# The last keys of four batches packed into three V tiles, and the output projections of attention 1 one round sooner

## The chip, the cores and the metric

The kernel runs on one core of a Trainium2 chip. The metric is the device time of one execution in microseconds (us). The engines are named as in the profile: PE (TensorE, matrix products), PEld (its weight loads), DVE (VectorE), ACT (ScalarE), POOL (GpSimd) and SP (SyncE, which here only issues DMAs). Each engine runs its own list of instructions in order and waits on semaphores.

## The reference, cut to what matters

Two layers of gated cross attention and feed-forward act on x, which is 8 batches x 100 rows x 512. The keys and values come from a context of 8 batches x 722 keys x 512, with 16 heads of width 32.

```
k = heads(ctx @ Wk.T + bk)         # 722 keys a batch
v = heads(ctx @ Wv.T + bv)
p = softmax(q @ k.T / sqrt(32))    # attention 0 adds a mask
x = x + tanh(g) * (p @ v)          # attention 1: (p @ v) @ Wo.T + bo
x = x + tanh(f) * ffn(layernorm(x))
```

722 keys are five tiles of 128 and one of 82.

## The kernel before

The program runs attention 0, a ternary feed-forward of 88 weight units, attention 1 and a quantized feed-forward of 7 row tiles. Products of fp32 numbers are made from a high and a low half in the type fp32r: high by high, high by low and low by high, so one product over 512 inputs is 4 x 3 = 12 matmuls.

**Rounds.** Each attention works through 64 pairs of heads, 8 for each batch. In round i PE issues `scores(i+1)` (four matmuls, lines 850 to 855), `turn(i)` (twelve transposes of the weights of pair i, L866), the jobs of `beside(i)`, and `weigh(i-1)` (six matmuls of the turned weights with V, L888; L881 in the last batch of attention 0). The table `BESIDE` at line 64 says which jobs stand in which of the 8 rounds of a batch. A job `("v", x, kt)` makes tile kt of V for the batch x further on (L806, 128 keys as the stationary operand, 512 moving columns). A job `("k", x, g, half)` makes a part of the keys (L802). Before the change, the first entry is `(("v", 0, 5), ("k", 0, 3, 1))`: the tile of the last 82 keys of this batch, then a K job.

**The other engines in round i.** DVE: `peak` twice (L1293, the maxima of the scores), `low_weighed(i-2)` (L1314, L1318), `low_turned(i)` (L1299, three pieces), then the low halves of the jobs (`low_job`, L1281 for K, L1285 for V). ACT: `high_weighed(i-2)` (L1845), `high_turned(i)` (L1830), `weights` twice (L1818, exponentials) and the high halves of the jobs (`high_job`, L1786 and L1799). A job's PSUM bank comes out of a ring of two banks which it shares with `weigh` and others. `ring_free` waits until the item two places back has been read. The second score matmul of a round waits for both exponentials of the round before. POOL makes the low halves of the context (L2179). SP issues the loads in an order written out by hand.

**Extras in attention 0.** From round 17 on, in rounds with i % 8 = 1, PE turns a normalized batch (`turn_normal`, L929), DVE runs `low_weighed` ahead of `peak`, and `normal_out` (L1416) stands at the end of the round before.

**The end of attention 1.** `OUT_AT` at line 126 puts `project(n)` (12 matmuls with Wo, L1003) for row tiles n = 0 to 5 into rounds 58 to 63, where no jobs are left. Around it stand ACT `high_out(n)` (L1861), POOL `low_out(n)` (L2205), POOL `add_bo(n)` (L2212), DVE `add_projected(n)` (L1349, which waits for `project(n)` and for `add_bo(n)`) and `stats_projected(n)` (L1357, L1359). POOL splits Wo beforehand (`high_wo`, `low_wo`, L2197 and L2200). DVE `scale_rows(n)` (from L1370 or L1375) prepares the quantized rows. `turn_rows(0)` (L1015) is the first step of the feed-forward on PE. It stands in round 63 and waits for the second piece of `low_turned(63)`, and the rest of PE's list stands behind it.

## Time and profile before

| | |
|---|---|
| median of 3 runs | 1589.43 us (1589.24 to 1590.16) |
| the profiled execution's own time | 1589.02 us |
| its span in the trace | 1587.1 us |
| PE, PEld | 1572.9 us (99%), 1431.8 us (90%) |
| DVE, ACT, POOL | 1021.3 us (64%), 968.2 us (61%), 401.6 us (25%) |
| chain that ended last | PE 92%, DVE 4%, DMA 2% |

"Busy" is the time covered by at least one record of the engine. Records of matmuls overlap, so what a matmul costs is the time from its start to the start of the next one. A line of the timeline has the start in us, the duration, the engine, the source line, the operation, what it writes and reads, the shape and a count. In brackets stands the idle time of the engine before it and what ended it.

### The profile page before, as it was taken

The numbers are of one execution on the slowest core, as the hardware profiler recorded it, in microseconds if no ns is written. First come the engines' busy times: TensorE is split into PE (matmuls) and PEld (weight loads), VectorE is DVE, ScalarE is ACT, GpSimd is POOL, SyncE is SP. The second block draws the span as 40 slices with busy tenths as digits, with TensorE's granted clock in tenths as the row PEclk, the third lists the DMA queues.
The fourth block names the chain that finished last, engine by engine and source line by source line (L and its number), as shares of the span: only waits on it lengthen the run. The fifth ranks groups of instructions, "written<-read, shape, count | busy, mean of one in ns | idle before, by whom it ended". The sixth has DMA issues, their size and how long they took to land.

```text
span 1587.1 us, 25783 instructions
## 1 busy us (share of the span) xinstructions
PE 1572.9 (99%) x9370; PEld 1431.8 (90%) x9370; DVE 1021.3 (64%) x1807; ACT 968.2 (61%) x2006; POOL 401.6 (25%) x545
## 2 busy tenths in 40 slices
PE   9999999999999999999999999999999999999999
PEld 7899899989988999999999998889989889998765
DVE  6577787787785562223544425647777777777987
ACT  5566767677765455544544435357667667766676
POOL 4111211212144222222222222311102111113751
PEclk9999999999999999999999999999999999999999
DMA  8766776676582325554375643576676676658500
GB/s 249 176 166 173 184 187 180 156 201 174 140 209 85 105 81 194 175 190 160 104 230 193 221 156 97 171 183 183 151 195 164 163 178 176 177 132 222 183 13 30
DMA packets 146966, 258.15 MB, mean 163 GB/s; under 512 B 40944, under 2 KB 91248, under 8 KB 146701
## 3 DMA queue, kind: packets, MB, share of 16 engines
q1 hardware_dynamic: 146497, 256.10, 57.7%
q8 instruction: 86, 1.41, 0.4%
q14 instruction: 51, 0.42, 0.1%
q10 hardware_dynamic: 332, 0.23, 0.0%
HBM read 187.86 MB, written 58.57 MB: 155 GB/s over the span
## 4 chain that ended last, share of the span: by engine, by line
PE 92%; DVE 4%; DMA 2%; issue 1%; ACT 1%; SPq 0%; POOL 0%; DVEq 0%; ACTq 0%
PE ps L1152 33%; PE ps L806 17%; PE ps L802 15%; PE ps L888 8%; PE ps L866 8%; PE ps L1086 2%; PE ps L954 2%; PE ps L850 2%; PE ps L855 2%; PE ps L1103 1%; PE ps L853 1%; PE ps L854 1%; PE ps L1003 1%; DMA KS<-kd 1%; DVE PT L1299 1%
## 5 line engine op out<-in xcount | busy, mean ns | idle before, releaser
L1152 PE MATMUL ps<-ah_f,wh_f 128*128 128x400 f32 (+1 forms) x1296 | 442.9, 343 | 0.0
L1152 PE MATMUL ps<-al_f,wh_f 128*128 128x400 f32 (+1 forms) x1296 | 442.2, 342 | 0.0
L2179 POOL TENSOR_TENSOR cxl<-raw,cxh 128x384 fp32r<-128x384 f32 (+1 forms) x112 | 105.7, 965 | 613.8 <-ACT cxh L1775 613.8
L1697 DVE TENSOR_TENSOR wl_f<-raw_f,wh_f 128x1024 fp32r<-128x1024 f32 x85 | 103.7, 1223 | 232.7 <-POOL wh_f L2169 232.6
L1152 PEld LDWEIGHTS ps<-al_f,wh_f 128*128 128x128 f32 x1296 | 243.8, 188 | 0.0
L1152 PEld LDWEIGHTS ps<-ah_f,wh_f 128*128 128x128 f32 x1296 | 243.5, 188 | 0.1
L1293 DVE TENSOR_REDUCE nmax<-ps 100x1 f32<-100x722 f32 x256 | 220.7, 903 | 32.5 <-PE ps L854 29.1
L1818 ACT ACTIVATE P<-ps,nmax 100x722 f32<-100x722 f32 x256 | 220.2, 862 | 29.7 <-DVE nmax L1293 29.4
L1830 ACT ACTIVATE PT<-ps 128x400 fp32r<-128x400 f32 x384 | 165.9, 505 | 70.6 <-PE ps L866 69.5
L2097 ACT ACTIVATE raw_f<-wl_f 128x1024 f32<-128x1024 f32 x88 | 93.4, 1061 | 174.6 <-DVE wl_f L1697 174.5
L1299 DVE TENSOR_TENSOR PT<-ps,PT 128x400 fp32r<-128x400 f32 x384 | 196.3, 566 | 4.3 <-ACT PT L1830 1.1
L2169 POOL CAST wh_f<-raw_f 128x1024 fp32r<-128x1024 f32 x85 | 92.8, 1092 | 334.4 <-PE ps L1152 323.7
L802 PE MATMUL ps<-cxh,wkh 128*128 128x338 f32 (+1 forms) x512 | 173.3, 338 | 0.7 <-DVE cxl L1271 0.7
L802 PE MATMUL ps<-cxh,wkl 128*128 128x338 f32 (+1 forms) x512 | 168.4, 329 | 0.0
L802 PE MATMUL ps<-cxl,wkh 128*128 128x338 f32 (+1 forms) x512 | 167.6, 327 | 0.0
L806 PE MATMUL ps<-wvh,cxh 128*128 128x512 f32 (+1 forms) x384 | 159.1, 414 | 0.9 <-DVE V L1281 0.9
L866 PE MATMUL ps<-ident,P 100*128 100x100 f32 (+1 forms) x1536 | 153.1, 249 | 1.3 <-DVE PT L1299 1.3
L866 PEld LDWEIGHTS ps<-ident,P 100*128 100x128 f32 (+1 forms) x1536 | 143.0, 137 | 12.0 <-ACT P L1818 1.5
L888 PE MATMUL ps<-PT,V 128*128 128x400 f32 x720 | 150.9, 344 | 0.6 <-DVE ksl L1281 0.6
L806 PE MATMUL ps<-wvh,cxl 128*128 128x512 f32 (+1 forms) x384 | 151.1, 393 | 0.0
L806 PE MATMUL ps<-wvl,cxh 128*128 128x512 f32 (+1 forms) x384 | 150.6, 392 | 0.0
L1281 DVE SCALAR_TENSOR_TENSOR ksl<-ps,cols,ksh 128x384 fp32r<-128x384 f32 (+1 forms) x120 | 71.0, 591 | 112.9 <-ACT ksh L1786 112.9
(218 smaller groups left out, 2592.3 us busy)
## 6 DMA issues: line engine op xcount, KB each, us to landing
KS<-kd SPq DMA_DIRECT2D x192, 361.0 KB
raw_f<-in_h SPq DMA_DIRECT2D x64, 512.0 KB, 4.5
raw_f<-in_gud SPq DMA_DIRECT2D x48, 512.0 KB, 4.6
raw<-in_ctx SPq DMA_DIRECT2D x64, 192.0 KB, 3.7
raw_f<-in_w SPq DMA_DIRECT2D x24, 512.0 KB, 3.7
kd<-ksh SPq DMA_DIRECT2D x60, 192.0 KB, 2.2
kd<-ksl SPq DMA_DIRECT2D x60, 192.0 KB, 2.5
raw<-in_ctx SPq DMA_DIRECT2D x64, 169.0 KB, 4.2
```

What stands on the lines that cost most here:

```text
L802: ins = e.matmul(o, m.wk[x][:, k, 128 * j[2]:128 * j[2] + 128], m.cx[y][:, k, off:off + n], start=(k == 0 and c == 0), stop=(k == 3 and c ...
L806: ins = e.matmul(o, m.cx[y][:, k, 128 * kt:128 * kt + KM[kt]], m.wv[x][:, k, :], start=(k == 0 and c == 0), stop=(k == 3 and c == 2))
L866: ins = e.transpose(ps[0:KM[kt], bank, o:o + S], m.P[0:S, (2 * i + h) % 3, 128 * kt:128 * kt + KM[kt]], ident[0:S, 0:S])
L888: ins = e.matmul(o, m.V[b % 2][0:r, kt, g, 128 * pr:128 * pr + 128], m.PT[0:r, i % 2, :, kt, :], start=(kt == 0), stop=(kt == KT - 1))
L1152: return e.matmul(o, p, q, start=start, stop=stop)
L1293: e.tensor_reduce(m.nmax[0:S, c:c + 1], scores_of(n), AX.X, ALU.max, negate=True).then_inc(v_max, 1)
L1299: e.tensor_tensor(lo, ps[:, bank, 0:400].rearrange("p (k n) -> p k n", k=2), raw32(hi), ALU.subtract).then_inc(v_t, 1)
L1697: e.tensor_tensor(wl[:, z, :], raw[:, r, :], raw32(wh[:, z, :]), ALU.subtract).then_inc(v_ul, 1)
L1818: e.activation(m.P[0:S, n % 3, :], scores_of(n), ACT.Exp, bias=m.nmax[0:S, c:c + 1], accum_out=m.rs[0:S, r:r + 1]).then_inc(a_exp, 1)
L1830: e.activation(m.PT[:, i % 2, 0, 2 * x:2 * x + 2, :], ps[:, bank, 0:400].rearrange("p (k n) -> p k n", k=2), ACT.Copy).then_inc(a_t, 1)
L2097: e.activation(raw[:, r, :], raw32(wl[:, z, :]), ACT.Abs, accum_out=low[:, z, 0:1]).then_inc(a_raw, 1)
L2179: e.tensor_tensor(m.cx[1][:, k, off:off + n], m.raw[:, k, off:off + n], raw32(m.cx[0][:, k, off:off + n]), ALU.subtract).then_inc(g_cx, 1)
```

## The change

1. The job `("v", 0, 5)` leaves the first round of a batch. In the second round (i % 8 = 1) a new `tail_job` stands ahead of `("v", 1, 0)`, for batches with b % 4 < 3. Its stationary operand of 114, 128 or 114 keys holds the last keys of this batch and of the next one (`PIECES`), so four batches need three jobs. `weigh(8b)`, the last step of the same round, waits for it.
2. The host lays the tails out in a new input. SP loads a tile (`load_tail`, 128 x 512 numbers) in the last round of the batch before, POOL splits it in the first round (`split_tail`, a cast and a subtraction), ACT and DVE write the result to V in two pieces each (`high_tail`, `low_tail`), since the rows go to two V buffers. From batch 1 on, the tile stands in the buffer of the raw context. SP therefore waits for the tail job before it loads the context of batch b + 2.
3. `OUT_AT` starts at round 57. `STATS_AFTER`, `OUT_FIRST`, the root and normalization steps on POOL and `scale_rows` on DVE move by one round with it. POOL's `add_bo(0)` and `add_bo(1)` stay in round 57.

```diff
-BESIDE = [(("v", 0, 5), ("k", 0, 3, 1)),
+BESIDE = [(("k", 0, 3, 1),),
+def tail_at(i):
+    return i // 8 if i < NP and i % 8 == 1 and i // 8 % 4 < 3 else None
+PIECES = (((0, 0, 0, 82), (96, 1, 64, 82)),
+          ((0, 0, 0, 64), (64, 1, 0, 64)),
+          ((96, 0, 64, 82), (0, 1, 0, 82)))
+TAIL_ROWS = (114, 128, 114)
...
-OUT_AT = {58 + i: i for i in range(TILES - 1)}
-STATS_AFTER = (59, 60, 61)
-OUT_FIRST = (60, 62)
+OUT_AT = {57 + i: i for i in range(TILES - 1)}
+STATS_AFTER = (58, 59, 60)
+OUT_FIRST = (59, 61)
...
+                    if p == 7 and tail_at(i + 2) is not None:
+                        load_tail(L, m, b + 1)
...
                     if p in (1, 5) and b + 2 < B:
+                        if p == 1 and b:
+                            w.wait_ge(p_job, tail_done(L, b))
...
+                def tail_job(b):
+                    j = ("v", b, KT - 1)
+                    ring_free(j)
+                    w.wait_ge(g_tail, 2 * (6 * L + tail_of(b)) + 2)
+                    r, o = TAIL_ROWS[b % 4], job_out(m, j, ring_bank(L, j))
+                    for k in range(4):
+                        wait_low_w(w, L, 4 + k)
+                        n = 128 * (k % 2)
+                        for c, (x, y) in enumerate(PAIRS):
+                            ins = e.matmul(o, m.tail[min(b, 1)][y][:, k // 2, n:n + r], m.wv[x][:, k, :],
+                                           start=(k == 0 and c == 0), stop=(k == 3 and c == 2))
+                    ins.then_inc(p_job, 1)
...
-                    w.wait_ge(v_job, NJOB * L + JOB[L]["v", b, KT - 1] + 1)
+                    w.wait_ge(v_job, tail_done(L, b))
...
+                def low_tail(b):
+                    j = ("v", b, KT - 1)
+                    w.wait_ge(a_job, NJOB * L + JOB[L][j] + 1)
+                    for v, o in tail_parts(m, b, ring_bank(L, j)):
+                        ins = e.tensor_tensor(v[:, :, 1:3, :], o, raw32(v[:, :, 0:4:3, :]), ALU.subtract)
+                    ins.then_inc(v_job, 1)
...
-                    if L and i == 61:
+                    if L and i == 60:
                         scale_rows(0)
+                    if L and i == 62:
+                        scale_rows(1)
                     if L and i == 63:
                         inverse(B - 1)
-                        scale_rows(1)
...
-                    if L and i == 60:
+                    if L and i == 59:
                         normal(0)
-                    if L and i == 62:
+                    if L and i == 61:
                         quantize(0)
                     if L and i + 1 in OUT_AT:
                         low_out(OUT_AT[i + 1])
-                    if L and i == 60:
+                    if L and i == 59:
                         tile_roots(1)
                     if L and i == 57:
                         add_bo(0)
-                    if L and (57 <= i < 61 or i == 62):
-                        add_bo(min(i - 56, 5))
+                        add_bo(1)
+                    if L and 58 <= i < 62:
+                        add_bo(i - 56)
...
+                def high_tail(b):
+                    j = ("v", b, KT - 1)
+                    w.wait_ge(p_job, NJOB * L + JOB[L][j] + 1)
+                    w.wait_ge(p_pv, NP * L + 8 * b)
...
+                    for v, o in tail_parts(m, b, ring_bank(L, j)):
+                        ins = e.activation(v[:, :, 0:4:3, :], o, ACT.Copy)
+                    ins.then_inc(a_job, 1)
...
+                def split_tail(b):
+                    (high, low), new = m.tail[min(b, 1)], m.tail_raw[min(b, 1)]
+                    w.wait_ge(d_tail, 16 * (6 * L + tail_of(b) + 1))
+                    if b:
+                        wait_ctx(w, L, b + 1, 0, 3)
+                    e.tensor_copy(high, new).then_inc(g_tail, 1)
+                    w.wait_ge(g_tail, 2 * (6 * L + tail_of(b)) + 1)
+                    e.tensor_tensor(low, new, raw32(high), ALU.subtract).then_inc(g_tail, 1)
...
-                    w.wait_ge(p_job, 2 * NJOB - 1)
+                    w.wait_ge(p_job, NJOB + JOB[1]["v", B - 1, KT - 2] + 1)
```

**Where instructions move.** The first place is DVE in rounds 16 and 17 of attention 0, before: from the maxima of round 16 to the end of round 17.

```order
138 L1293 TENSOR_REDUCE nmax_57<-ps 100x1 x2
139 L1314 TENSOR_TENSOR sum_65<-ps,sum_65 64x200
140 L1318 TENSOR_TENSOR QT_68<-ps,sum_65 32x100 x2
141 L1299 TENSOR_TENSOR PT_64<-ps,PT_64 128x2x200 x3
142 L1285 TENSOR_TENSOR V_0_60<-ps,V_0_60 82x4x128
143 L1281 SCALAR_TENSOR_TENSOR ksl_72<-ps,cols,ksh_71 128x338
144 L1416 TENSOR_SCALAR x_100<-x_100,mv,rq 100x512
145 L1314 TENSOR_TENSOR sum_65<-ps,sum_65 64x200
146 L1318 TENSOR_TENSOR QT_68<-ps,sum_65 32x100 x2
147 L1293 TENSOR_REDUCE nmax_57<-ps 100x1 x2
148 L1299 TENSOR_TENSOR PT_64<-ps,PT_64 128x2x200 x3
149 L1285 TENSOR_TENSOR V_0_61<-ps,V_0_61 128x4x128
```

The same place after the change, from the K job of round 16 on.

```order
144 L1347 SCALAR_TENSOR_TENSOR ksl_72<-ps,cols,ksh_71 128x338
145 L1490 TENSOR_SCALAR x_108<-x_108,mv,rq 100x512
146 L1388 TENSOR_TENSOR sum_65<-ps,sum_65 64x200
147 L1392 TENSOR_TENSOR QT_68<-ps,sum_65 32x100 x2
148 L1367 TENSOR_REDUCE nmax_57<-ps 100x1 x2
149 L1373 TENSOR_TENSOR PT_64<-ps,PT_64 128x2x200 x3
150 L1359 TENSOR_TENSOR V_0_60<-ps,V_0_60 18x4x128
151 L1359 TENSOR_TENSOR V_0_61<-ps,V_0_61 82x4x128
152 L1351 TENSOR_TENSOR V_0_61<-ps,V_0_61 128x4x128
```

The 82-row piece has left round 16, and two pieces of 18 and 82 rows stand in round 17 behind the maxima.

The second place is POOL in rounds 56 to 58 of attention 1, before.

```order
387 L2197 CAST woh<-wos 128x512 x4
388 L2200 TENSOR_TENSOR wol<-wos,woh 128x512 x4
389 L2205 TENSOR_TENSOR otl_116<-QT_93,oth_115 128x460
390 L2212 TENSOR_TENSOR xr<-xr,bo_123 115x512 x2
391 L2205 TENSOR_TENSOR otl_118<-QT_93,oth_117 128x460
392 L2212 TENSOR_TENSOR xr<-xr,bo_123 115x512
```

And after the change.

```order
411 L2301 CAST woh<-wos 128x512 x4
412 L2304 TENSOR_TENSOR wol<-wos,woh 128x512 x4
413 L2309 TENSOR_TENSOR otl_124<-QT_97,oth_123 128x460
414 L2309 TENSOR_TENSOR otl_126<-QT_97,oth_125 128x460
415 L2316 TENSOR_TENSOR xr<-xr,bo_131 115x512 x2
```

The low half of output tile 1 now stands between that of tile 0 and the addition of the bias to rows 0 and 1.

The third place is DVE behind the turned weights of rounds 62 and 63 of attention 1. Before, from the turned weights of round 63 on.

```order
1008 L1299 TENSOR_TENSOR PT_89<-ps,PT_89 128x2x200 x3
1009 L1327 RECIPROCAL rr_80<-rs_81 100x16
1010 L1370 TENSOR_SCALAR hs<-xr,mv,rq 115x512
1011 L1375 TENSOR_REDUCE ax<-hs 115x1
1012 L1377 TENSOR_SCALAR ax<-ax 115x1
1013 L1378 TENSOR_SCALAR ax<-ax 115x1
1014 L1380 RECIPROCAL ax<-ax 115x1
1015 L1382 TENSOR_SCALAR ax<-ax,tot 115x1 x2
1016 L1384 TENSOR_SCALAR ax<-ax 115x1
1017 L1349 SCALAR_TENSOR_TENSOR xr<-ps,gt,xr 115x512
1018 L1357 BN_STATS st<-xr 115x6
1019 L1359 BN_AGGR mv<-st 115x2
```

After the change, from the first step behind the turned weights of round 62 up to those of round 63.

```order
1015 L1449 TENSOR_REDUCE ax<-hs 115x1
1016 L1451 TENSOR_SCALAR ax<-ax 115x1
1017 L1452 TENSOR_SCALAR ax<-ax 115x1
1018 L1454 RECIPROCAL ax<-ax 115x1
1019 L1456 TENSOR_SCALAR ax<-ax,tot 115x1 x2
1020 L1458 TENSOR_SCALAR ax<-ax 115x1
1021 L1423 SCALAR_TENSOR_TENSOR xr<-ps,gt,xr 115x512
1022 L1431 BN_STATS st<-xr 115x6
1023 L1433 BN_AGGR mv<-st 115x2
1024 L1388 TENSOR_TENSOR sum_94<-ps,sum_94 64x200
1025 L1392 TENSOR_TENSOR QT_97<-ps,sum_94 32x100 x2
1026 L1373 TENSOR_TENSOR PT_93<-ps,PT_93 128x2x200 x3
```

`scale_rows(1)`, `add_projected(5)` and its statistics have moved ahead of the turned weights of round 63.

## Rows read from the trace of the kernel before

**Rows 1.** The page: busy time, share and instructions of each engine

```profile
PE 1572.9 (99%) x9370; PEld 1431.8 (90%) x9370; DVE 1021.3 (64%) x1807; ACT 968.2 (61%) x2006; POOL 401.6 (25%) x545
```

**Rows 2.** Timeline of PE, attention 0: a K job of 338 columns, a V job

```profile
153.16 0.32 PE L802 MATMUL ps<-cxh,wkh 128*128 128x338 f32 x1
...
155.03 1.25 PE L888 MATMUL ps<-PT,V 128*128 128x400 f32 x6
...
158.18 0.47 PE L806 MATMUL ps<-wvh,cxh 128*128 128x512 f32 x1
...
161.04 1.25 PE L888 MATMUL ps<-PT,V 128*128 128x400 f32 x6
```

**Rows 3.** Timeline of attention 1, round 9, which has one V job

```profile
1124.28 0.39 PE L850 MATMUL ps<-KS,QS 96*100 96x512 f32 x1
...
1124.90 1.73 DVE L1293 TENSOR_REDUCE nmax<-ps 100x1 f32<-100x722 f32 x2 [0.37 <-PE ps L854]
...
1127.52 0.86 ACT L1818 ACTIVATE P<-ps,nmax 100x722 f32<-100x722 f32 x1
1127.64 1.54 DVE L1299 TENSOR_TENSOR PT<-ps,PT 128x400 fp32r<-128x400 f32 x3
...
1128.77 1.26 PE L888 MATMUL ps<-PT,V 128*128 128x400 f32 x6
1128.97 0.60 ACT L1799 ACTIVATE V<-ps 128x512 fp32r<-128x512 f32 x1 [0.51 <-PE ps L806]
1129.60 0.69 DVE L1285 TENSOR_TENSOR V<-ps,V 128x512 fp32r<-128x512 f32 x1 [0.42 <-ACT V L1799]
1129.87 0.40 PE L850 MATMUL ps<-KS,QS 96*100 96x512 f32 x1
```

**Rows 4.** Timeline of attention 1, rounds 57 and 58: the second score matmul waits

```profile
1460.89 0.85 ACT L1818 ACTIVATE P<-ps,nmax 100x722 f32<-100x722 f32 x1
...
1461.89 0.34 PE L853 MATMUL ps<-KS,QS 96*100 96x210 f32 x1 [0.37 <-ACT P L1818]
```

**Rows 5.** Timeline of attention 0, rounds 0 to 2

```profile
59.18 0.39 PE L850 MATMUL ps<-KS,QS 98*100 98x512 f32 x1
...
60.62 1.72 DVE L1293 TENSOR_REDUCE nmax<-ps 100x1 f32<-100x722 f32 x2
...
65.17 1.76 ACT L1775 ACTIVATE cxh<-raw 128x384 fp32r<-128x384 f32 x4
...
71.65 0.39 PE L850 MATMUL ps<-KS,QS 98*100 98x512 f32 x1
```

**Rows 6.** Timeline of DVE, attention 0, rounds 16 and 17

```profile
177.18 0.54 DVE L1416 TENSOR_SCALAR x<-x,mv,rq 100x512 f32<-100x512 f32 x1
...
178.73 1.73 DVE L1293 TENSOR_REDUCE nmax<-ps 100x1 f32<-100x722 f32 x2
```

**Rows 7.** Timeline of attention 1, rounds 56 to 58, around the first output tile

```profile
1450.23 0.40 PE L850 MATMUL ps<-KS,QS 96*100 96x512 f32 x1
...
1457.32 5.00 POOL L2200 TENSOR_TENSOR wol<-wos,woh 128x512 fp32r<-128x512 f32 x4
...
1462.39 1.09 POOL L2205 TENSOR_TENSOR otl<-QT,oth 128x460 fp32r<-128x460 f32 x1
...
1463.44 2.55 POOL L2212 TENSOR_TENSOR xr<-xr,bo 115x512 f32<-115x512 f32 x2
```

**Rows 8.** Stretch: length; busy PE, PEld, DVE, ACT, POOL; clock, DMA share, GB/s

```profile
1467.50:1484.60 17.10, 17.10 (x108) 14.60 (x107) 16.14 (x34) 12.78 (x31) 14.01 (x29) 1.00 0.95 323
```

**Rows 9.** Timeline of DVE and PE, attention 1, rounds 58 to 64

```profile
1466.63 0.75 DVE L1349 SCALAR_TENSOR_TENSOR xr<-ps,gt,xr 115x512 f32<-115x512 f32 x1
...
1495.96 0.36 PE L1015 MATMUL ps<-idb,xq 115*128 115x115 bf16 x4
...
1496.37 0.46 DVE L1370 TENSOR_SCALAR hs<-xr,mv,rq 115x512 f32<-115x512 f32 x1
...
1499.96 0.33 DVE L1314 TENSOR_TENSOR sum<-ps,sum 64x200 f32<-64x200 f32 x1
```

More of the change, by code:

```diff
@@ L438, in job_out @@
                 return ps[:, bank, 0:HALF[j[3]][1]]
-            return ps[0:KM[j[2]], bank, :]
+            return ps[0:TAIL_ROWS[j[1] % 4] if j[2] == KT - 1 else KM[j[2]], bank, :]
         def ring_bank(L, item):
@@ L2352, in attention @@
                 low_q(0)
+                split_tail(0)
                 low_ctx(1, 0)
@@ L2355, in attention @@
                     b, p = divmod(i, 8)
+                    if i and tail_at(i + 1) is not None:
+                        split_tail(b)
                     if scaled_at(i + 1) is not None:
@@ L2457, in col @@
         return v.reshape(-1, 128).T
+    tails = np.zeros((6, 128, 4, 128), np.float32)
+    for b in range(B):
+        for o, x, r0, r1 in PIECES[b % 4] if b % 4 < 3 else ():
+            keys = I["ctx_1024"][b + x, 640 + r0:640 + r1, :]
+            tails[tail_of(b), :, :, o:o + r1 - r0] = keys.reshape(r1 - r0, 4, 128).transpose(2, 1, 0)
+    tails = tails.reshape(6, 128, 512)
     a = {
```

63 lines of the change are left out of this document (51 added, 12 removed).

## The prediction, made before the changed kernel was run

> **What bounds the kernel now.** I read the page first: PE has a record in work for 99% of the span [rows 1], so time comes off only where PE has less to do. The records overlap, so I priced PE's work by starts. A V job runs from 158.18 to 161.04, where the next kind of matmul starts: 2.86 us for 12 matmuls, of which 0.07 is a longer first slot that its successor has anyway. I take 2.8 us, or 0.23 us a matmul. The 338-column K job takes 155.03 - 153.16 = 1.87 us, and I take 1.84 [rows 2]. The stationary operand may be 82 keys or 128, the 512 columns stream either way.
>
> Then I read one round as a clock, from its first score matmul [rows 3]. The maxima start at +0.62 and end at +2.35. The second exponential runs from +3.24 to +4.10. `weigh` starts at +4.49 behind one V job and the next round at +5.59. So scores and turns take 4.49 - 2.8 = 1.69 us and `weigh` 1.10. A round without jobs would take PE 2.8 us, but the exponentials end at +4.10, so about 4.1 us is the least length of a round. PE starts 0.15 us after the exponential it waited for: 1461.89 against 1460.89 + 0.85 [rows 4]. With these two numbers I see which round becomes too short.
>
> Last comes the end of attention 1. There DVE is busy 16.14 of 17.10 us [rows 8]. It is as much a bound there as PE.
>
> **What is removed.** Per attention 8 tail jobs become 6, so 4 jobs go: 4 x 2.8 = **-11.2 us**. The Trainium skill (TensorE: Matmul & The Clock Gate, Back-to-back issue gap) gives 131 ns per matmul of 512 columns as a sustained rate. By it the four jobs would be worth 4 x 12 x 0.131 = 6.3 us (an estimate by that page). The trace has 0.23 us for this very matmul, and the trace decides.
>
> **Rounds with i % 8 = 0** lose 2.8 us and keep the K job: 1.69 + 1.84 + 1.10 = 4.63 us, above 4.1. They still cover the exponentials, by 0.5 us. `weigh` starts at +3.53 here, and its bank is free when DVE has done `low_weighed`. That one ends where the turned weights start: 1127.64 - 1124.28 = +3.36 [rows 3], plus 0.15 makes 3.51. It just fits. I take 0, with up to 0.1 in each of 14 rounds (+1.4) as the upper bound.
>
> **Tail rounds (i % 8 = 1).** The tail job ends at +4.49, the V job behind it at +7.29, then `weigh` waits for the tail. ACT starts its first piece at +4.69 (0.20 after the job, as 1128.97 against 1128.77), the second 0.49 later, and ends at +5.78. DVE starts at +5.81 and needs two pieces, 0.61 + 0.69 since neighbours overlap by 0.08: +7.11. With 0.15 PE is free at +7.26, against +7.29 [rows 3]. I price a piece of 18 rows like one of 128, as rows do not shorten these operations. So 0 for the six plain cases (batches 1, 2, 4, 5, 6 of attention 1 and batch 1 of attention 0), with up to 0.2 each (+1.2) as the upper bound. POOL's two new operations and SP's load end well ahead: the split takes about 2 us in a round in which POOL has nothing else, and SP's new wait delays only a context load that is used five rounds later.
>
> The Trainium skill (GPSIMD Engine Reference, 1. Specifications) says that POOL shares its SBUF interfaces with VectorE, with contention for DVE instructions with two SBUF inputs. The DVE steps of a round read at least one operand from PSUM, so I put no price on it.
>
> **Attention 0, batches 2, 4, 5 and 6.** `normal_out` used to start 0.18 after the next round's scores (177.18) and the maxima at 178.73, 1.73 after them [rows 6]. In the shorter round it follows the K job and starts at 5.25 - 4.64 = +0.61 of the next one. The maxima end at 0.61 + 1.55 + 1.73 = +3.89, the exponentials with the accumulator's read-out at +5.73. Now ACT is late for the tail: pieces until +6.82, DVE until +8.15, PE free at +8.30. `weigh` is due at 7.29 + 0.34 for the extra transposes = 7.63. That is 0.67 each: **+2.7 us** (0 to 3.6).
>
> **Batch 0 of both attentions.** The maxima of round 1's scores start late, at 60.62 - 59.18 = +1.44, behind a V piece, and end at +3.16 [rows 5]. The exponentials end at 3.16 + 0.03 + 0.85 + 0.86 = +4.90, so the second score matmul comes at +5.05. Without V job and `weigh`, PE gets there at 1.69 + 1.84 + 0.23 = +3.76. It waits 1.3 us. Behind the exponentials ACT has the K copy, four context copies (1.76, [rows 5]), about 1.3 for the turned weights and two exponentials, until +10.4. The tail's copies end at +11.5, DVE's at +12.8, PE goes on at +12.95, while it was due at +12.2. The round after starts at 12.95 + 1.10 = 14.05. Before, it was 71.65 - 59.18 = 12.47 with the same number of jobs. So +1.6 each, **+3.1 us** (1 to 4).
>
> **The last batch of attention 0.** Round 56 shrinks as well and `normal_out` delays the first maximum by 0.45 us, in a stretch whose rounds are bounded by the exponentials: **+0.5 us** (0 to 1).
>
> **The end of attention 1.** I count from the scores at 1450.23. Before: the first `add_projected` starts at 1466.63 (+16.4) and `turn_rows(0)` at 1495.96 (+45.7) [rows 7, 9]. These 29.3 us are DVE's work.
> - After, round 57 starts at +4.64. POOL finishes Wo about 2.5 us sooner than before, as the V tile that it waits for is no longer last: 1462.32 - 1450.23 - 7.3 = +4.8 (before it started behind the tail job, now behind the scaling of bo). The low half of tile 0 ends near +6.6 and PE waits 0.35 us for it.
> - Tile 1's high half comes behind the exponentials of round 57, until +9.6. POOL needs 1.09 for its low half and only then adds the bias to row tile 0, 1.3: +12.0 [rows 7]. `add_projected(0)` waits for that and DVE stands still for 2.4 us.
> - From +12.05 DVE has the 29.3 us of before, one more round of maxima, weighed and turned pieces (1129.18 - 1124.90 = 4.3, [rows 3]), and `scale_rows(1)` with `add_projected(5)` and its statistics (1499.96 - 1496.37 = 3.6, [rows 9]), which used to stand behind. That makes +49.2 for `turn_rows(0)`, with PE idle for some 5 us before it.
>
> So this stretch is 3.5 us longer, though it holds 2.8 us less of V job. Behind it PE was the bound, and at most 0.1 comes back. Stall: 3.5 + 2.8 - 0.1 = **+6.2 us** (3 to 7.5).
>
> **Sum.** -11.2 + 2.7 + 3.1 + 0.5 + 6.2 = +1.3 us on the profiled execution's 1589.0: 1590.3. The median of the runs lies 0.4 above that execution, so I predict **1590.7 us**.
>
> **Rivals.**
> - *The tail is paid for, no more.* DVE catches up at the end, or POOL's bias step is not what holds it, so that 6.2 shrinks to 1 or less, and the smaller waits stay: -11.2 + 2.7 + 3.1 + 0.5 + 1 = -3.9, 1585.5. With half of the smaller waits gone as well, about 1582.5. For it: PE was busy 17.10 of 17.10 us in the stretch [rows 8], so something there did fit around DVE. Against it: DVE's share. Chance 0.27.
> - *The thin margins open (the slower side).* In the rounds of 4.63 us `low_weighed` decides at 3.51 against 3.53, in the tail rounds DVE's second piece at 7.26 against 7.29. From 0.05 us of delay on, each such round stalls. At 0.1 and 0.2 that is 1.4 + 1.2 = 2.6, with the end at its upper bound 1.3 more: 1594.6. Chance 0.25.
> - *A matmul is cheaper than its slot*, so that removing one gives 0.131 us: -6.3 instead of -11.2, 1595.6. The spacing in [rows 2] is steady and without idle time, which speaks against it. It is the rule of the Trainium skill's page named above. Chance 0.01.
> - *The change does not do what it says*, for instance because PE starts waiting for `split_tail`. POOL is free and the load has a full round, so 0.01 more on the slower side.
>
> **Numbers.** My forecast, 1590.7, has 0.46. Its own range is 1587 to 1592.6. The range for eight in ten reaches to 1584 below (the first rival without its far end) and to 1595 above (the second). A measurement of this kernel can tell about 0.2% (3.2 us) from no change. Faster by more than that (below 1586.2) 0.27, within it 0.46, slower (above 1592.6) 0.27.
>
> **What would show it.** V rows of L806's kind should drop by 48 matmuls. Rounds with i % 8 = 0 should last 4.6 us. In attention 0, `weigh` should wait about 0.7 us for DVE in rounds 17, 33, 41 and 49. The waits of PE should have a new row of 4 to 5 us, `turn_rows(0)` behind DVE's turned weights. DVE should stand idle for 2 us or so before its first `add_projected`, released by POOL's bias step. If that last wait is missing, the forecast is too high by up to 6 us. If `weigh` waits in every tail round, it is too low.

## The result, and the profile after

The changed kernel takes 1597.26 us (median of 6 runs, 1595.13 to 1599.51). The kernel before took 1588.92 us (median of 6 runs, 1588.36 to 1590.16). The ratio is 1.0055, with a 95% interval of 1.0044 to 1.0066. So it is slower, by 8.3 us as the two medians have it (8.7 by the ratio). The prediction was 1590.7 us with a range of 1584 to 1595, so the measured time lies above the range. The profiled execution took 1597.67 us, its span in the trace is 1595.3 us, 8.2 us more than before.

The page of the changed kernel, busy time of each engine (answers [rows 1]):

```profile
PE 1568.5 (98%) x9322; PEld 1430.1 (90%) x9322; DVE 1026.4 (64%) x1815; ACT 971.1 (61%) x2014; POOL 424.0 (27%) x569
```

PE has 48 matmuls fewer (9322 against 9370) and is busy 4.4 us less than before, yet the span grew by 8.2. So PE waits where it did not wait before. The view of waits of PE shows where. Its two longest rows and that of the tails, over the whole span (what waits, what it waits for, us in total, times, longest):

```profile
PE ps L1079 <- DVE PT L1373: 5.0, 1, 5.0
PE ps L1067 <- DVE xr L1423: 2.8, 2, 2.2
...
PE ps L952 <- DVE V L1359: 1.7, 6, 0.4
```

`turn_rows(0)` waits 5.0 us for DVE's turned weights, as forecast. `project(1)` waits 2.2 us for DVE's first `add_projected`, which was not forecast. `weigh` waits for the tail in six rounds so long that PE stands idle. In the other six tail rounds it starts late as well, but by so little that the record before it still covers the wait (below).

Now the end of attention 1, from the scores at 1450.64 on (before they start at 1450.23, [rows 7]). KS is the tile of keys that the scores read, and it comes from memory through `kd`. PE:

```profile
1450.64 0.40 PE L914 MATMUL ps<-KS,QS 96*100 96x512 f32 x1
...
1465.49 0.48 PE L1067 MATMUL ps<-woh,oth 128*115 128x512 f32 x1 [2.25 <-DVE xr L1423]
...
1466.17 0.63 PE L1067 MATMUL ps<-woh,otl 128*115 128x512 f32 x1
1466.60 0.63 PE L1067 MATMUL ps<-woh,oth 128*115 128x512 f32 x1
...
1501.74 0.55 PE L1079 MATMUL ps<-idb,xq 115*128 115x115 bf16 x4 [4.99 <-DVE PT L1373]
...
1508.78 1.44 PE L952 MATMUL ps<-PT,V 128*128 128x400 f32 x6
```

DVE, POOL and SP's queue in the same stretch:

```profile
1464.68 0.75 DVE L1423 SCALAR_TENSOR_TENSOR xr<-ps,gt,xr 115x512 f32<-115x512 f32 x1 [4.48 <-POOL xr L2316]
```

```profile
1460.08 1.09 POOL L2309 TENSOR_TENSOR otl<-QT,oth 128x460 fp32r<-128x460 f32 x1 [2.76 <-ACT oth L1953]
1463.32 2.49 POOL L2316 TENSOR_TENSOR xr<-xr,bo 115x512 f32<-115x512 f32 x2 [2.15 <-DMA xr<-xs]
```

```profile
1454.61 1.27 SPq L747 DMA_DIRECT2D KS<-kd  x3
1455.92 0.43 SPq L729 DMA_DIRECT2D kd<-ksh  x1
1456.39 0.43 SPq L729 DMA_DIRECT2D kd<-ksl  x1
1456.87 2.54 SPq L670 DMA_DIRECT2D xr<-xs  x4
```

DVE stands still for 4.48 us, released by POOL's bias step. The prediction had this wait, with 2.4 us. But POOL itself had finished the low half of tile 1 at 1461.17 and then waited 2.15 us for a DMA: its bias step could start only 6.45 us after the issue of the rows of x at 1456.87. Before, POOL came to this step at 1463.44, behind other work and without a wait [rows 7], so the landing could not be seen.

The view by stretches tells the rest. The columns are those of [rows 8]; PEclk is the last figure but two.

```profile
1467.00:1469.00 2.00, 2.00 (x6) 1.50 (x5) 1.90 (x6) 0.96 (x3) 1.50 (x7) 0.50 1.02 215
...
1501.00:1503.00 2.00, 1.26 (x7) 1.28 (x8) 1.24 (x4) 0.56 (x1) 0.70 (x2) 0.50 0.00 0
1503.00:1505.00 2.00, 2.00 (x7) 1.52 (x6) 0.19 (x1) 0.33 (x1) 1.92 (x2) 0.50 0.04 8
```

Behind both waits of PE the granted clock is 0.50, which is the lower of the two levels (1.2 GHz against 2.4), and matmuls of 512 columns start 0.43 us apart (1466.60 against 1466.17) instead of 0.23. Behind `turn_rows(0)` PE has a `weigh`, the first 16 products of the feed-forward and a second `weigh`. From the start of `turn_rows(0)` to that second `weigh` it takes 1508.78 - 1501.74 = 7.04 us. Before it took 4.61 (1495.96 to 1500.57):

```profile
1495.96 0.36 PE L1015 MATMUL ps<-idb,xq 115*128 115x115 bf16 x4
...
1500.57 1.45 PE L888 MATMUL ps<-PT,V 128*128 128x400 f32 x6
```

A plain tail round of the changed kernel, attention 1, round 9 (before: [rows 3]):

```profile
1123.09 0.39 PE L914 MATMUL ps<-KS,QS 96*100 96x512 f32 x1
...
1124.72 0.71 PE L872 MATMUL ps<-wvh,tail 128*128 128x512 f32 x2
...
1130.12 0.39 PE L856 MATMUL ps<-wvl,cxh 128*128 128x512 f32 x1
1130.44 1.36 PE L952 MATMUL ps<-PT,V 128*128 128x400 f32 x6
1131.65 0.40 PE L914 MATMUL ps<-KS,QS 96*100 96x512 f32 x1
```

```profile
1127.77 1.20 ACT L1891 ACTIVATE V<-ps 64x512 fp32r<-64x512 f32 x2 [0.50 <-PE ps L872]
```

```profile
1129.00 1.39 DVE L1359 TENSOR_TENSOR V<-ps,V 64x512 fp32r<-64x512 f32 x2 [1.02 <-ACT V L1891]
```

The last V matmul starts at 1130.12, so `weigh` is due 0.23 later, at 1130.35. It starts at 1130.44, 0.05 after DVE's second piece (1129.00 + 1.39 = 1130.39). It then takes 1.21 us instead of 1.10.

Measured against the steps of the prediction, in us, on the two profiled executions (each line is the sum over its rounds of the time from scores to scores, after minus before):

| part | forecast | measured |
|---|---|---|
| six plain cases: round i % 8 = 0 without, next round with a tail job | 0 | +1.4 |
| attention 0, batches 2, 4, 5, 6 | +2.7 | +3.0 |
| batch 0 of both attentions | +3.1 | +2.4 |
| batch 3 of both attentions: a job less, no tail | -5.6 | -5.4 |
| last batch of attention 0: a job less, the rest | -2.3 | -1.6 |
| attention 1, scores at 1450 to `turn_rows(0)`, a job less | +3.5 | +5.4 |
| behind `turn_rows(0)` | -0.1 | +2.4 |
| other rounds, which the change does not touch | 0 | +0.6 |
| sum | +1.3 | +8.2 |

The +0.6 of the other rounds is in three of them: round 21 of attention 0 (+0.4) and rounds 29 and 53 of attention 1 (-0.7 and +1.0). These lengths differ between profiles of the same code: round 53 took 7.8 us in the changed kernel, and 7.0, 7.1 and 7.5 in the kernels of the first, seventh and eighth experiment.

### The profile page after: what moved, and what is told of

It is laid out like the page before. It is cut to its first block, busy times and chain, and to the rows that moved or that the text cites. A ratio compares the mean times of both kernels' runs of the same rounds, so it can differ in the third digit from the quotient of the medians.

```text
span 1595.3 us, 25762 instructions
## 1 busy us (share of the span) xinstructions
PE 1568.5 (98%) x9322; PEld 1430.1 (90%) x9322; DVE 1026.4 (64%) x1815; ACT 971.1 (61%) x2014; POOL 424.0 (27%) x569
## 3 DMA queue, kind: packets, MB, share of 16 engines
q8 instruction: 85, 1.39, 0.4%
## 4 chain that ended last, share of the span: by engine, by line
PE 86%; DVE 7%; ACT 3%; DMA 2%; issue 1%; POOL 1%; SPq 0%; DVEq 0%; ACTq 0%
PE ps L1218 32%; PE ps L852 14%; PE ps L856 13%; PE ps L952 8%; PE ps L930 6%; PE ps L1152 2%; PE ps L1018 2%; PE ps L914 2%; PE ps L919 1%; DVE nmax L1367 1%; DVE PT L1373 1%; PE ps L1169 1%; PE ps L872 1%; ACT P L1910 1%; PE ps L917 1%
## 5 line engine op out<-in xcount | busy, mean ns | idle before, releaser
L952 PEld LDWEIGHTS ps<-PT,V 128*128 128x128 f32 x720 | 130.1, 189 | 11.0 <-DVE V L1359 6.5
L856 PE MATMUL ps<-wvh,cxh 128*128 128x512 f32 x320 | 131.5, 411 | 0.9 <-DVE V L1347 0.9
L856 PE MATMUL ps<-wvh,cxl 128*128 128x512 f32 x320 | 126.0, 394 | 0.0
```

The lines of the kernel that those rows point to most:

```text
L856: ins = e.matmul(o, m.cx[y][:, k, 128 * kt:128 * kt + KM[kt]], m.wv[x][:, k, :], start=(k == 0 and c == 0), stop=(k == 3 and c == 2))
L952: ins = e.matmul(o, m.V[b % 2][0:r, kt, g, 128 * pr:128 * pr + 128], m.PT[0:r, i % 2, :, kt, :], start=(kt == 0), stop=(kt == KT - 1))
```

## Experiments

The theory after the result: the tails pay for themselves; the end of attention 1 is what costs the time, through DVE's list, the late rows of x, and the half clock behind PE's waits. The runs take these apart. Ratios are to the kernel before, run on the same chip.

**The tails alone.** The changed kernel with `OUT_AT` and all that moved with it back in their places.

```diff
-OUT_AT = {57 + i: i for i in range(TILES - 1)}
-STATS_AFTER = (58, 59, 60)
-OUT_FIRST = (59, 61)
+OUT_AT = {58 + i: i for i in range(TILES - 1)}
+STATS_AFTER = (59, 60, 61)
+OUT_FIRST = (60, 62)
```

> The packed tail tiles stay, the output projections of attention 1 are back in rounds 58 to 63 with all that moved with them. Theory A (the tails pay for themselves and a little more, the end is what cost the time): up to the scores of round 56 of attention 1 the changed kernel's trace is 0.4 us behind, its round 56 is 2.7 us shorter, and DVE's first add_projected can start at the end of the bias step, 1464.6 us, against 1466.63 before. From there to turn_rows(0) DVE has its 29.3 us as before. So 2.0 us less than before: 1587.0 us (1585.5 to 1588.5). Theory B (the sum of the prediction without its term for the end is right): 1589.0 - 11.2 + 6.3 + 0.4 = 1584.5 us. Theory C (the tail rounds cost more than the four jobs are worth, also at the end): 1590 us or more.

Measured: 1587.26 us (11 runs), ratio 0.9988 (0.9979 to 0.9997). The tails are worth about 2 us, and the end is what turned this into a loss. `turn_rows(0)` comes 43.5 us after the scores of round 57 (1493.73 - 1450.22), against 45.7 before and 51.1 in the changed kernel, and no wait stands before it. DVE's first `add_projected` is held by the bias step here too, but for 0.60 us only:

```profile
1464.60 0.75 DVE L1423 SCALAR_TENSOR_TENSOR xr<-ps,gt,xr 115x512 f32<-115x512 f32 x1 [0.60 <-POOL xr L2315]
```

**The sooner output projections alone.** The kernel before with the same three tables moved to 57, 58 and 59, and the steps that moved with them.

> The kernel before, with only the third part of the change: output projections, their statistics, roots, normalization and scaling one round sooner; the jobs for the last 82 keys as before. Theory A: DVE's first add_projected is held by the rows of x from memory and the bias step, about 1464.7 us, and the work from there to turn_rows(0) is the 37.1 us that the changed kernel showed (1464.68 to 1501.74), so turn_rows(0) comes at 1501.8 us, 5.8 later than before, and a half clock behind it costs 2.4 more: 1589.4 + 8.2 = 1597.6 us (1595 to 1599). Theory B (only a short round 56 makes the sooner projections a loss; behind a long one they fit): no more than 1590 us.

Measured: 1600.35 us (5 runs), ratio 1.0064 (1.0050 to 1.0078). A loss without any tail, so rival B falls. It is 3 us above A, and the trace says why: `project(0)` waits 3.9 us for POOL, which could split Wo only behind the last V job of round 56.

```profile
1457.42 4.98 POOL L2201 TENSOR_TENSOR wol<-wos,woh 128x512 fp32r<-128x512 f32 x4
1462.36 2.12 POOL L2206 TENSOR_TENSOR otl<-QT,oth 128x460 fp32r<-128x460 f32 x2
```

```profile
1463.54 0.70 PE L1003 MATMUL ps<-woh,oth 128*115 128x512 f32 x1 [3.93 <-POOL otl L2206]
...
1505.38 0.55 PE L1015 MATMUL ps<-idb,xq 115*128 115x115 bf16 x4 [5.00 <-DVE PT L1299]
```

DVE's first `add_projected` starts at 1468.13 and `turn_rows(0)` 37.25 us later. In the changed kernel these are 1464.68 and 37.06 us. So DVE's list between the two has a fixed length, whatever released its start. That the change lets POOL split Wo sooner is a part of it that helps.

**POOL's order alone.** This tests the step of the prediction.

```diff
+                    if L and i == 57:
+                        add_bo(0)
                     if L and i + 1 in OUT_AT:
                         low_out(OUT_AT[i + 1])
...
                     if L and i == 57:
-                        add_bo(0)
                         add_bo(1)
```

> The changed kernel with POOL's add_bo(0) ahead of low_out(1) in round 57. The prediction's theory (DVE's first add_projected waits because POOL does the low half of tile 1 first): the bias step ends 1.1 us or more sooner, and up to 2.4 us come back, 1595 us. Theory A (the rows of x are not there before 1463.3 us, and the low half of tile 1 had ended at 1461.2): nothing comes back, the low half of tile 1 ends 3 us later and project(1) starts behind it, about 1465.6 instead of 1465.49: within 0.5 us of the changed kernel, 1597.3 us.

Measured: 1598.32 us (5 runs), ratio 1.0057 (1.0044 to 1.0071). Nothing comes back. `turn_rows(0)` stands at +51.5, against +51.1 in the changed kernel. POOL's order by itself is not what held DVE, since the rows of x were not there yet.

**PE kept busy before `turn_rows(0)`.**

```diff
                     if L and i == NP - 1:
+                        w.wait_ge(v_id, 1)
+                        w.wait_ge(d_wb[0], 32)
+                        for _ in range(22):
+                            e.matmul(ps[:, 2, :], idb[:, :], down_block(0)[:, 0:512], start=True, stop=True)
                         turn_rows(0)
```

> The changed kernel with 22 matmuls of 512 columns on constant data, written to a free bank, between the last transposes and turn_rows(0): they do nothing but keep PE busy for about 4.7 of the 5.0 us that it waits. Theory A (the granted clock of 0.50 from 1501 to 1506 us is what the wait leaves behind, and it cost 7.04 - 4.61 = 2.4 us between turn_rows(0) and the second weigh behind it): the clock stays at 1.00 there and the time falls by 2.4 us, to 1594.9. Rival (the slow stretch is something else, such as the weights' arrival, or the time behind it has slack): no change, or slower if the filling ends after DVE's turned weights.

Measured: 1596.28 us (5 runs), ratio 1.0044 (1.0030 to 1.0057). A said 1594.9, and the median gained 1.0 of the 2.4 us. The trace shows the effect without the scatter between executions:

```profile
1497.55 4.91 PE L1102 MATMUL ps<-wb,idb 128*128 128x512 bf16 x22
1502.71 0.36 PE L1079 MATMUL ps<-idb,xq 115*128 115x115 bf16 x4 [0.25 <-DVE PT L1377]
1502.89 1.33 PE L952 MATMUL ps<-PT,V 128*128 128x400 f32 x6
...
1507.33 1.45 PE L952 MATMUL ps<-PT,V 128*128 128x400 f32 x6
```

`turn_rows(0)` to `weigh` is 1507.33 - 1502.71 = 4.62 us again, against 7.04, and the granted clock is 1.00 from 1502 to 1508. So the 2.4 us behind `turn_rows(0)` are the half clock that PE's wait leaves. The medians alone (1597.3 and 1596.3) would not have settled it. This profile has a stretch of half clock in attention 0 (from 474.5 to 477.9 us) that the changed kernel's has not, so the two spans differ by 1.4 us only.

**`scale_rows(1)` back behind `low_turned(63)`.**

```diff
-                    if L and i == 62:
-                        scale_rows(1)
                     if L and i == 63:
                         inverse(B - 1)
+                        scale_rows(1)
```

> The changed kernel with DVE's scale_rows(1) behind low_turned(63), where it was before. Theory A (the last wait of PE is DVE's list, step by step): the 2.05 us from 1495.79 to 1497.84 leave the path, turn_rows(0) comes 2.0 us sooner, PE still waits 2.9 us and the granted clock still falls to 0.50 behind it, as it did behind a wait of 2.25 us: 1597.5 - 2.0 = 1595.5 us. If a wait of 2.9 us is short enough to keep the clock, 2.4 more: 1593.1. Rival (POOL's quantize(1), which now comes later, becomes the wait of turn_rows(1)): no change.

Measured: 1596.08 us (5 runs), ratio 1.0043 (1.0029 to 1.0056). PE's wait falls from 5.0 to 2.9 us, as A says, and the clock still falls behind it (`weigh` takes 2.35 us, 1.33 at the full clock):

```profile
1501.07 0.54 PE L1079 MATMUL ps<-idb,xq 115*128 115x115 bf16 x4 [2.95 <-DVE PT L1373]
1501.38 2.35 PE L952 MATMUL ps<-PT,V 128*128 128x400 f32 x6
```

**Row tile 0 loaded ahead of the two stores of the last K job.**

```diff
+                    if L and i == 56:
+                        w.wait_ge(p_pv, NP + 56)
+                        load_rows(0)
                     for j in beside(i):
                         if j[0] == "k":
                             store_k(L, m, *j[1:])
```

> The changed kernel with the load of row tile 0 ahead of the two stores of the last K job, that is about 1 us sooner and ahead of their data. Theory A (the landing of these rows holds the bias step, and with it DVE and PE): the bias step starts 1 to 2 us sooner, as does everything up to turn_rows(0), and the time falls by 1 to 2 us, 1596 us. Rival (the rows would be there, POOL waits for something else, or they land no sooner because the queue is full of the KS load issued at 1454.61): no change.

Measured: 1597.32 us (5 runs), ratio 1.0050 (1.0037 to 1.0064): no change. A's number was wrong. Counted from the scores, the rows were issued only 0.3 us sooner (at +5.95 instead of +6.23), since the KS load ahead of them went out later in this run (+4.6 instead of +4.0). And POOL still starts 6.5 us after their issue (1457.69 to 1464.20), though no store stands between them and the KS load any more. So the stores are not what they queue behind:

```profile
1456.38 1.27 SPq L749 DMA_DIRECT2D KS<-kd  x3
1457.69 0.43 SPq L672 DMA_DIRECT2D xr<-xs  x1
```

```profile
1464.20 1.27 POOL L2318 TENSOR_TENSOR xr<-xr,bo 115x512 f32<-115x512 f32 x1 [1.56 <-DMA xr<-xs]
```

**The tails alone, with a signal of its own for ACT's first piece.**

```diff
 def low_tail(b):
-    w.wait_ge(a_job, NJOB * L + JOB[L][j] + 1)
-    for v, o in tail_parts(m, b, ring_bank(L, j)):
+    w.wait_ge(a_tail, 6 * L + tail_of(b) + 1)
+    for x, (v, o) in enumerate(tail_parts(m, b, ring_bank(L, j))):
+        if x:
+            w.wait_ge(a_job, NJOB * L + JOB[L][j] + 1)
...
 def high_tail(b):
-        ins = e.activation(v[:, :, 0:4:3, :], o, ACT.Copy)
-    ins.then_inc(a_job, 1)
+        e.activation(v[:, :, 0:4:3, :], o, ACT.Copy).then_inc(a_job if x else a_tail, 1)
```

The new semaphore takes the place of the one for the row of the bias of V, whose step now counts on another one.

> The kernel with the tails alone, with a signal of its own for ACT's first piece of a tail, so that DVE takes the first piece while ACT does the second. Theory A (in every tail round weigh waits for DVE's second piece, and each such wait, even of 0.08 us, also costs weigh's first slots 0.11): DVE ends 0.6 us sooner, which gives 0.2 in each of the six plain rounds, 0.6 in the four of attention 0 with the late maxima and 0.6 in the two of batch 0: -4.8, from 1587.3 to 1582.5 us. Rival (the 0.2 us of a plain tail round is not a wait but the price of the tail's matmuls with a new weight tile of 114 or 128 rows): only the four and the two rounds gain, -3.6 or less, 1583.7 us or more.

Measured: 1583.86 us (6 runs), ratio 0.9965 (0.9953 to 0.9977). In the trace the six plain tail rounds are 0.20 to 0.22 shorter, four of attention 0 0.52 to 0.61, and those of batch 0 0.44. That is 4.4 us. The median alone, 1583.86, would fit the rival (1583.7 or more), but the rival has nothing for the plain tail rounds, and they gained what A said. The profile also shows a loss of 1.4 us at the end, of a kind that the next runs are about. The same tail round as above, now with no gap before `weigh`, 8.36 us long instead of 8.56:

```profile
1120.23 0.39 PE L914 MATMUL ps<-KS,QS 96*100 96x512 f32 x1
...
1127.49 1.26 PE L952 MATMUL ps<-PT,V 128*128 128x400 f32 x6
1128.59 0.40 PE L914 MATMUL ps<-KS,QS 96*100 96x512 f32 x1
```

```profile
1125.54 1.39 DVE L1361 TENSOR_TENSOR V<-ps,V 64x512 fp32r<-64x512 f32 x2 [0.41 <-ACT V L1892]
```

**The same, with `normal_out` in the tail round behind the turned weights and `turn_normal` one round later.**

```diff
-    return i // 8 - 2 if i % 8 == 1 and 16 < i < NP else None
+    return i // 8 - 2 if i % 8 == 2 and 16 < i < NP else None
...
-                    if L == 0 and 8 < i < NP - 8 and i % 8 == 0:
+                    if L == 0 and i % 8 == 1 and 16 < i:
                         normal_out(i // 8 - 2)
```

The steps that belong to these two in the last batch of attention 0 move by a round as well.

> The same with attention 0's normal_out in the tail round behind the turned weights, and turn_normal one round later, so that the maxima of the tail round are not late. Theory A (the late maxima come from normal_out at the start of the round): together with the two signals nothing of the 0.7 us waits is left; as the two signals alone take 0.6 of it, another 0.1 to 0.2 in each of four rounds, -0.6: 1582.0 us. Rival (low_weighed ahead of the maxima in the next round costs as much there): 1582.5 us or more.

Measured: 1584.08 us (6 runs), ratio 0.9969 (0.9957 to 0.9981), no gain over the run beside it. The tail rounds are 0.44 to 0.54 us shorter, and the rounds behind them 0.33 longer, which leaves 0.1 to 0.2 for each batch, as A said. The last batch takes it back: from the scores of round 57 to those of round 63 PE needs 31.0 us in this profile, against 28.6 in the run beside it, with the clock at 0.50 for 6.8 us of it. Whether the edit causes this loss or only this execution had it, one profile does not tell.

**Rows of tiles 0 and 1 ahead of the KS load, without and with the bias step first.**

```diff
+                    if L and i == 56:
+                        w.wait_ge(p_pv, NP + 56)
+                        for n in range(2):
+                            load_rows(n)
                     if p in (0, 2):
                         load_k(L, m, b, 2 + p // 2)
```

> The changed kernel with the loads of row tiles 0 and 1 ahead of the KS load of round 56 on SP. Behind that load's data they landed 6.5 us after their issue. Theory A (the rows' landing holds the bias step; what they queue behind is the KS load): they are issued 1.5 us sooner and land within 3 us, so the bias step follows the low half of tile 1, which ends 10.5 us after the scores at 1450.6, and ends at +11.8 instead of +14.0. The wait of project(1) for add_projected(0) goes, with the half clock behind it, and turn_rows(0) comes 2.2 us sooner, with its 5.0 us wait unchanged: 1595.2 us. Rival (the landing takes 6 us wherever the load stands): about 1 us less at most, 1596.5 us.

> The same with add_bo(0) ahead of low_out(1) as well. The prediction had POOL's order as the wait of DVE; alone it changed nothing, since the rows were late. Theory A (two gates in a row: first the rows, then POOL's order): now the order counts. add_bo(0) ends about 9 us after the scores at 1450.6, and add_projected(0) starts when project(0) ends, at +10.1 instead of +14.0. turn_rows(0) comes 3.9 us sooner than in the changed kernel: 1593.5 us. Rival (with the rows in time POOL's order is worth nothing): as the run beside it, 1595.2 us.

Measured: 1594.30 us (5 runs), ratio 1.0039 (1.0025 to 1.0053), and 1594.76 us (5 runs), ratio 1.0034 (1.0021 to 1.0048). In the traces `turn_rows(0)` comes 49.1 and 47.2 us after the scores of round 57, against 51.1: 2.0 and 3.9 us sooner, where A said 2.2 and 3.9. In the second, POOL's bias step follows the issue of the rows by 2.7 us (1456.01 to 1458.73) and DVE waits for `project(0)` only:

```profile
1456.01 0.79 SPq L673 DMA_DIRECT2D xr<-xs  x2
1456.91 1.31 SPq L750 DMA_DIRECT2D KS<-kd  x3
```

```profile
1458.73 1.29 POOL L2319 TENSOR_TENSOR xr<-xr,bo 115x512 f32<-115x512 f32 x1 [0.75 <-DMA xr<-xs]
```

```profile
1461.15 0.75 DVE L1426 SCALAR_TENSOR_TENSOR xr<-ps,gt,xr 115x512 f32<-115x512 f32 x1 [0.22 <-PE ps L1070]
```

So there were two gates in a row, first the rows and then POOL's order. The prediction saw the second and not the first. The Trainium skill (DMA: Bandwidth & Descriptors, Queues, rings and completion order) says that on each DMA engine the descriptors of a queue are consumed in ring order. The two waits agree with it: 6.5 us behind the KS load, 2.7 us ahead of it. No run tells this order from a KS load that merely takes the bandwidth while the rows are under way.

The medians do not tell the second run from the first, and the traces say why. The second has a stretch of half clock in attention 0 that the first has not. And behind the same wait of 5.0 us the half clock cost different amounts: from `turn_rows(0)` to the end of the span the first takes 92.8 us, the second 94.1 and the changed kernel 93.5, where the kernels without that wait take 91.1 to 91.2. That is 1.7, 3.0 and 2.4 us. In the first, the clock had fallen sooner in the wait (at 1496.0, 3.3 us before `turn_rows(0)`) and was up again 3.5 us behind `turn_rows(0)`; in the second it fell 0.6 us before and stayed low for 6.2 us behind.

**PE kept busy in the short rounds at the end of each attention.** The kernel with tails and two signals, with six small matmuls behind `weigh`, in a bank that `ring_free` declares free.

```diff
                     if i:
                         weigh(i - 1)
+                    if i == 57 or L == 0 and 57 < i < 62:
+                        keep_busy(i)
```

> The kernel with the tails and two signals, with six matmuls of 256 columns on constant data behind weigh in round 57 of attention 1 and rounds 57 to 61 of attention 0, written to a bank of the ring that is free. In its profile the granted clock was 0.50 for some 3 us behind round 57 of attention 1, in others at the same place of attention 0, and project(0) took 1.3 us longer; the kernel before never showed it. Theory A (the short rounds at the end leave PE waiting, and the waits take the clock): the clock stays at 1.00 there, the median falls by about 1.3 us to 1582.5, and the runs lie closer together. Rival (the fillings themselves delay the scores, or the clock falls all the same): 1583.9 us or more.

> The same with the loads of row tiles 0 and 1 ahead of the KS load. In the kernel with the tails alone DVE waited 0.6 us for the bias step before add_projected(0), and the rows held that. Theory A: that wait goes, and DVE's work up to turn_rows(0), which is the path there, starts 0.6 us sooner: 1581.9 us. Rival (add_projected(0) then waits for project(0), which ends no sooner): no change against the run beside it, 1582.5 us.

Measured: 1583.39 us (5 runs), ratio 0.9966 (0.9952 to 0.9979), and with the rows loaded first 1583.57 us (7 runs), ratio 0.9969 (0.9958 to 0.9980). The clock is 1.00 throughout both last batches. `project(0)` of attention 1 is quick again: its round takes 5.89 us against 7.87 with two signals alone, where PE had waited 0.96 and 0.37 us and the stretch behind read

```profile
1455.00:1460.00 5.00, 4.63 (x23) 3.75 (x23) 4.90 (x11) 4.43 (x12) 1.68 (x2) 0.67 1.02 312
```

But the median gained only 0.5. In attention 0 the first filling waited for its bank:

```profile
461.27 0.83 PE L904 MATMUL ps<-ident 128*128 128x256 bf16 x6 [1.28 <-ACT QT L1967]
```

Loading the rows first gave nothing here, as its rival said: `add_projected(0)` starts at +13.6 us in both, and DVE does not stand idle before it.

**Two last runs**, on what was still open: the filling without that one place, and the changed kernel with all three causes at its end mended (rows first, bias step first, 22 matmuls before `turn_rows(0)`).

> The kernel with tails, two signals and fillings, without the filling of round 57 in attention 0. There the filling waited 1.28 us for ACT's keep_normal to free the bank of the ring, and the round took 7.2 us instead of 5.4. Theory A (that wait, not the filling as such, is what the fillings cost): the round is 5.4 us again, the clock stays at 1.00, and the time falls by 1.3 to 1.8 us, from 1583.4 to 1581.9 us. Rival (the next rounds give the time back, since the exponentials bound them, or the clock falls without this filling): 1583 us or more.

> The changed kernel with all three causes at the end of attention 1 mended: rows of tiles 0 and 1 loaded ahead of the KS load, add_bo(0) ahead of low_out(1), and 22 matmuls that keep PE busy before turn_rows(0). Theory A (the causes add: 3.9 and 2.4 us of 8.3): turn_rows(0) comes 47.2 us after the scores of round 57's start instead of 51.1, the clock stays at 1.00 behind it, and the time is 1597.3 - 3.9 - 2.4 = 1591.0 us. The kernel with the tails alone needs 43.5 us there, so 3.7 us remain that are DVE's: the scaling, the last add_projected and its statistics ahead of the turned weights, now in front of PE. Rival (one hides the other, or the time behind turn_rows(0) has slack): 1593 us or more.

Measured: 1582.04 us (5 runs), ratio 0.9956 (0.9943 to 0.9970), where A said 1581.9. But the mechanism in the trace is the rival's. Round 57 takes 5.39 us again instead of 7.21, and the next five rounds give 1.6 of these 1.8 us back. The scores of round 57 start at 449.94 with that filling and at 449.98 without it, those of round 63 at

```profile
479.72 0.48 PE L921 MATMUL ps<-KS,QS 98*100 98x512 f32 x1
```

and at

```profile
479.54 0.48 PE L921 MATMUL ps<-KS,QS 98*100 98x512 f32 x1
```

So the traces show 0.2 us for this filling, and the 1.35 us between the two medians of 5 runs are not explained by it.

The second kernel: 1591.25 us (11 runs), ratio 1.0019 (1.0010 to 1.0028), where A said 1591.0. The two gates (3.9) and the half clock (2.4) thus add up; in the traces `turn_rows(0)` comes 4.05 us sooner than in the changed kernel, and what follows takes 2.4 us less. `turn_rows(0)` stands at +47.05 (1497.47 - 1450.42):

```profile
1497.47 0.36 PE L1082 MATMUL ps<-idb,xq 115*128 115x115 bf16 x4 [0.25 <-DVE PT L1380]
```

Even so mended, the sooner output projections are 4 us slower than the tails alone (1587.26). Of these, 47.05 - 43.5 = 3.5 us are lost up to `turn_rows(0)`. There DVE has 3.6 us of scaling, last `add_projected` and statistics in front of the turned weights that PE waits for.

The fastest of these kernels is the one at 1582.04 us: packed tails, output projections in their old rounds, a signal for each tail piece, and PE kept busy in the short rounds. What the fillings give is at the end of attention 1, where `turn_rows(0)` comes at +43.0 instead of +44.9 with the two signals alone. From the scores of round 57 of attention 0 to those of round 1 of attention 1 they change nothing (610.3 against 610.2 us).

## Why the prediction was wrong

The forecast had the two long waits at the end of attention 1 in the right places, and the terms that it had costed for attention 0 were near. It missed a gate (the rows of x), the half clock that a wait of PE leaves behind, and a small wait in every plain tail round.

**What held.** A V job costs its slots: the 14 shortened rounds behind batch 0 lost 2.72 to 2.78 us each, where the step said 2.8, and the 0.131 us a matmul of the rival are out. The late maxima in attention 0 cost 0.67 to 0.84 us a batch (forecast 0.67), batch 0 1.2 (forecast 1.55). The 14 rounds of 4.63 us with a K job alone did not open; they took 4.67 to 4.71. DVE's list at the end was costed right: from the first `add_projected` to `turn_rows(0)` it grew from 29.3 to 37.06 us, by 7.7, and 4.3 + 3.6 = 7.9 was the forecast. `turn_rows(0)` waited for DVE's turned weights, about 5 us, as the forecast had it.

**Step 1 that failed, "POOL needs 1.09 for its low half and only then adds the bias ... +12.0".** The bias step ended at about +14.0. The step asked when POOL would be free, and not whether its other operand, the rows of x, would be there. The trace of before could not show a wait there, because POOL came late. But it had the issue of the load and the KS load around it, and the step passed over SP's queue. With the rows in time, POOL's order was worth the other 1.9 us, so the gate that the step did see is real; it is the second of two. The missed one cost 1.9 us more than forecast up to `turn_rows(0)`, and the run with the rows first brought 2.0 us back.

**Step 2 that failed, "Behind it PE was the bound, and at most 0.1 comes back".** The sum charged a wait of PE with its own length. The 5 us wait also left a half clock that cost 2.4 us behind it. The run that only fills this wait has the 2.4 us gone in its trace. The size is that of this profile: behind the same wait it was 1.7 us in one kernel and up to 3.0 in others.

**Step 3, a term of the wrong size: the plain tail rounds at 0.** They cost 0.24 each, 1.4 in all, a little more than the bound of 1.2 that the forecast gave them. It let the second piece start before the first had ended, 0.11 us on ACT and 0.08 on DVE. In the trace the two pieces follow each other without overlap: ACT took 1.20 us for them instead of 1.09, and DVE 1.39 instead of 1.30 with a first piece of 0.68 to 0.70 instead of 0.61. So DVE ended at +7.30, `weigh` started at +7.35, 0.09 after it was due, and took 0.11 longer itself. A margin of 0.03 us, worked out from terms that were out by 0.1 each, was no margin. The rival of the thin margins was right about these rounds and wrong about the rounds with i % 8 = 0. Its time, 1594.6, lies nearer to the result than the forecast by luck, since the time was lost at the end. So does that of the rival with the cheaper matmul, 1595.6, whose mechanism is out.

By the table the three are 1.9 + 2.5 + 1.4 = 5.8 of the 6.9 us by which the traces' difference exceeds the forecast. Of the rest, 0.6 is in rounds that the change does not touch, 0.7 in the last batch of attention 0, 0.3 in its batches with late maxima and 0.2 in batch 3; batch 0 came out 0.7 below its term.

**What stays open.** With the rounds shortened, PE waits more in the last batch of an attention. In six of the profiled kernels the granted clock fell there in attention 0, and one round took 6.0 us instead of 4.4, in one kernel 7.4. In others with the same code there it did not fall. The mean clock of every run is on record and shows that it differs between executions of one kernel, and that it goes with the time. Of the changed kernel's six runs, the one at 0.998 took 1595.1 us, the three at 0.997 took 1596.7 to 1597.7, and the two at 0.996 took 1599.5. So most of their spread of 4.4 us goes with how long the clock was low. The kernel before is not free of it: its profile shows no such stretch, but four of the 52 runs of it beside the experiments had a mean clock of 0.999. Nor is this all of the scatter, as fifteen of its runs, all at 1.000, spread over 3.5 us. Why the clock falls in one execution and not in the next no run shows.

## What to carry to other kernels

A step that is moved forward needs every operand forward. Look up when each one's transfer is issued and what stands ahead of it in its queue, even where the old trace shows no wait. A wait of PE of a few microseconds can cost more than its length, so a forecast that creates one should add the slow stretch behind it, priced from a stretch at the lower clock and with a range: here it was 1.7 to 3.0 us behind the same wait of 5.0. And a margin smaller than the error of the rows it is worked out from counts as used up: here a signal for each piece, which took 0.6 us off the handover, brought more (3.4 us) than the four removed jobs had (about 2). A last one: a median that comes out where the theory said is not yet the theory's mechanism; the kernel without the first filling hit its forecast to 0.1 us, and its trace shows another course.

## What was not expected of the hardware

- The granted clock fell to 0.50 behind waits of PE of 5.0, 2.95, 2.25 us and, in the kernel with two signals, behind two waits of 0.96 and 0.37 us only 0.5 us apart. The stretches at 0.50 were 3.4 us long, and 6.8 in every kernel with a wait of 5.0 us, where the clock fell before the wait was over. From `turn_rows(0)` on, 3.5 to 6.2 us of it were left, and they cost 1.7 to 3.0 us.
- Executions of one kernel differ in it: the six of the changed kernel had mean clocks of 0.996 to 0.998 and took 1599.5 down to 1595.1 us.
- The step that needs a 256 KB load of rows could start 6.5 us after the issue of that load behind a KS load (3 x 361 KB), and 2.7 us after it ahead of the KS load.
- When `weigh` had to wait at all, if only 0.1 us, it took 1.21 instead of 1.10 us itself (1130.44 to 1131.65; 1.19 to 1.21 in all twelve tail rounds), and 1.10 again where the wait was gone (1127.49 to 1128.59).
